# Graph network, pass 0: the last dense run's seven groups are summed from stored blocks instead of gathered rows

## The reference

```python
agg = segment_sum(x[src], dst)                    # pass 0
h1  = (agg + x) @ W1 + b1                         # 256 -> 1024
h1  = relu(batchnorm(h1) * gamma + beta)
x   = layernorm(x + relu(h1 @ W2 + b2))
deg = segment_sum(ones, dst) + 1                  # with self loops
for W, b in three layers:                         # passes 1 to 3
    h = relu(segment_sum((h @ W.T)[src] * norm, dst) + b)
out = layernorm(x + h)
```

## Time and profile before

| | |
|---|---|
| median of three runs | 2947.22 us |
| the profiled execution | 2956.98 us (its span 2955.2 us) |
| pass 0, up to the last chunk's copies | about 1106 us |
| network stage and three passes | the rest, about 1850 us |
| GpSimd in pass 0 | 832 gathers, eight per group |
| TensorE's granted clock over the span | 0.907 of full |

### The profile page before, as it was taken

The page is one execution under the profiler, slowest core; times in us unless marked ns, Lnnn a source line. Parts: engine busy times, 40 slices in busy tenths (PEclk is TensorE's granted clock), DMA queues, the critical chain, the costliest instruction groups (busy, mean ns, idle before and its releaser), DMA issues.

```text
span 2955.2 us, 44275 instructions
## 1 busy us (share of the span) xinstructions
PE 2422.4 (82%) x15812; PEld 1796.7 (61%) x15812; DVE 1422.1 (48%) x3544; ACT 956.6 (32%) x1512; POOL 2029.4 (69%) x2155
## 2 busy tenths in 40 slices
PE   3677766766676779989999987999999889999986
PEld 2444444444444457767777765777776667777764
DVE  7777787768687756751323133122222322324234
ACT  0111111111111115545444443444444344443430
POOL 6777777777777750027777776777777757777773
PEclk9987888878777879999999999999999999999997
DMA  4444554454455448987988898789898978888893
GB/s 135 137 160 143 162 159 143 160 159 159 143 162 160 142 136 272 345 282 258 321 284 290 275 335 279 243 263 306 275 309 303 316 238 263 271 272 272 259 331 105
DMA packets 361526, 681.74 MB, mean 231 GB/s; under 512 B 44243, under 2 KB 190633, under 8 KB 355403
## 3 DMA queue, kind: packets, MB, share of 16 engines
q0 software_dynamic: 103152, 296.88, 32.6%
q10 hardware_dynamic: 154688, 222.02, 22.8%
q1 hardware_dynamic: 103451, 159.81, 15.3%
HBM read 560.99 MB, written 117.51 MB: 230 GB/s over the span
## 4 chain that ended last, share of the span: by engine, by line
PE 62%; DVE 16%; DMA 9%; issue 8%; DVEq 2%; ACT 2%; SPq 0%; POOL 0%; ACTq 0%
PE ps L1058 30%; PE ps L922 9%; PE ps L904 7%; PE ps L960 6%; DVE vreg L1246 5%; DMA hbuf<-parts_d 4%; PE ps L970 4%; PE ps L1042 2%; PE ps L934 2%; DMA xs<-in_x_dram 2%; DMA xs<-x_d 2%; DVEq L1203 2%; DVE vreg L1233 1%; PE ps L947 1%; DVE vreg L1227 1%
## 5 line engine op out<-in xcount | busy, mean ns | idle before, releaser
L619 POOL DMA_INDIRECT ring<-table_d,idx x1248 | 1194.3, 957 | 443.8 <-issue 377.8
L1058 PE MATMUL ps<-wide,hbuf 128*128 128x512 f32 x4116 | 1044.1, 406 | 35.5 <-DMA hbuf<-parts_d 30.6
L619 POOL DMA_INDIRECT ring<-in_x_dram,idx x832 | 819.5, 985 | 265.9 <-issue 251.6
L1058 PEld LDWEIGHTS ps<-wide,hbuf 128*128 128x128 f32 x4116 | 763.4, 192 | 260.5 <-issue 57.0
L779 ACT CAST wide<-abuf 128x1024 fp32r<-128x1024 uint8 (+1 forms) x588 | 552.5, 940 | 636.5 <-PE ps L1058 636.5
L1199 DVE TENSOR_TENSOR acc<-acc,ps 128x256 f32 x260 | 107.6, 414 | 680.1 <-PE ps L922 678.3
L904 PE MATMUL ps<-ring,hot 128*32 128x256 f32 x4160 | 322.2, 432 | 103.0 <-issue 75.1
L922 PE MATMUL ps<-place,strips 128*128 128x128 f32 x2080 | 328.1, 308 | 66.5 <-ACT strips L666 36.2
L934 PE MATMUL ps<-vreg 128*128 128x300 bf16 x832 | 196.6, 348 | 223.0 <-DVE vreg L1246 204.0
L922 PEld LDWEIGHTS ps<-place,strips 128*128 128x128 f32 x2080 | 306.0, 219 | 107.5 <-ACT strips L666 55.9
L1246 DVE TENSOR_TENSOR vreg<-vreg,ps 128x600 f32 x416 | 326.2, 784 | 59.2 <-DVE vreg L1246 23.2
(11 more groups left out here) (131 smaller groups left out, 1541.2 us busy)
## 6 DMA issues: line engine op xcount, KB each, us to landing
hbuf<-parts_d ACTq DMA_DIRECT2D x84, 1024.0 KB
hbuf<-parts_d ACTq DMA_DIRECT2D x84, 768.0 KB
abuf<-ad_d ACTq DMA_DIRECT2D x63, 896.0 KB, 7.5
parts_d<-vreg SPq DMA_DIRECT2D x72, 512.0 KB, 5.4
h_d<-ureg SPq DMA_DIRECT2D x23, 1024.0 KB, 7.6
ureg<-h_d POOLq DMA_DIRECT2D x23, 1024.0 KB, 8.2
ad_d<-vreg SPq DMA_DIRECT2D x28, 784.0 KB, 4.2
ring<-table_d,idx POOLq DMA_INDIRECT x1248, 5.0
```

What stands on the lines that cost most here:

```text
L619: pool.indirect_dma_start(out=ring[:, i % SLOTS, j, :], out_offset=None, in_=table[0:N, :], in_offset=at).then_inc(g["rows"][i % SLOTS], 16)
L1058: ins = pe.matmul(ps[:, 2 + 4 * q + h, 0:(n1 - 4 * q) * P].rearrange("p (s n) -> p s n", n=P), hbuf[:, bl, e * D + h * P:e * D + (h + 1) * P],
```

## The change

Pass 0 no longer gathers the seven groups 84 to 90, the last dense run. Their sums come from the same four byte blocks that passes 1 to 3 use.

- The four blocks of that run are built first (`BORD`), so that they are stored early. The other 24 follow.
- `x` is split into upper and lower halves in pass 0: 49 pieces of 128 rows, two for each of the gathered groups 3 to 26 and one for group 27. SyncE loads a piece into `us`, VectorE masks and subtracts it (`split_x`, L1385 and L1388), and SyncE stores it to `xparts`.
- TensorE gets 196 steps (`quick_step`, L1083), four blocks by 49 pieces, one 128x512 matmul each into bank 5. They start at group 14, three in a turn (four in a block's first turn). The first is put ahead of the group's sums, the others behind the late tiles. ScalarE issues their loads (L835, L841) and widens the bytes (L848).
- The seven groups keep their place as turns in which only edges are counted. These are turns 23, 31, 42, 50, 61, 69 and 87 (`ORD`). In four of them (`QSUMS`) bank 5 is also copied and added to `acc` through matmuls with the identity. The 97 gathered groups stand at the turns `UNIT`.
- The 416 tile builds are spread over the 97 gathered groups. They keep their banks 2, 3, 6 and 7.
- Bank 5 is now the steps' in pass 0. So a group's strips and its sums share bank 4, and the edge counts go to bank 0, where every other pair of the hidden layer goes as well. The strips of a group must therefore wait until the group before has been added, which before only the counts behind the strips did.
- The degree row is kept in 16-bit integers. At the end of pass 0 it is loaded to `deg16`, and VectorE adds it into `deg` before TensorE transposes it.

```diff
+    QD = ND - 1
+    QGROUPS = list(range(*DENSE[QD]))
+    GATH0 = [k for k in range(NG) if k not in QGROUPS]
+    QSTART, QLEN = 14, 16
...
+    XSPLIT_AT = {UNIT[3 + b // 2]: list(range(b, min(b + 2, NB))) for b in range(0, NB, 2)}
...
+        SUMBANK, QBANK, COUNTBANK = (4, 5, 5, 5), 5, 0
...
+            for k in range(NG):
+                for b in XSPLIT_AT.get(k, ()):
+                    wait(sp, s_xst[b % 2], b // 2 * 16)
+                    sp.dma_start(xsplit(b)[0:xrows(b), D:HALVED * D], x[b * P:b * P + xrows(b), :]).then_inc(s_xq[b % 2], 16)
                 for t in BUILD_AT[k]:
                     if t in LAST:
                         store_block(LAST.index(t))
+                for b in XSPLIT_AT.get(k, ()):
+                    sp.wait_ge(s_xd, 2 * b + 2)
+                    sp.dma_start(xparts[b * P:b * P + xrows(b), :], xsplit(b)[0:xrows(b), :]).then_inc(s_xst[b % 2], 16)
...
             pool.wait_ge(s_idx, 2)
-            gather(0, x, EVERY)
+            gather(0, x, GATH0)
...
+            def quick_rows(q):
+                b = q % NB
+                wait(act, s_qstep, q - 2)
+                act.wait_ge(s_xst[b % 2], (b // 2 + 1) * 16)
+                act.dma_start(hq[:, q % 3, :].bitcast(F32), xparts[b * P:(b + 1) * P, :]).then_inc(s_qr[q % 3], 16)
+            def quick_widen(q):
...
+                wait(act, s_qstep, q - 1)
+                act.copy(wideq[:, q % 2, :], abq[:, n % 2, bl * P:(bl + 1) * P]).then_inc(s_qw, 1)
...
             def group_strips(a, i):
                 g = aggs[a]
                 pe.wait_ge(g["hot"], i + 1)
                 wait(pe, g["kept"], i)
                 if a == 0:
                     wait(pe, g["acc"], i)
+                if a > 0 or i in UNIT:
...
+                    wait(pe, fast[0]["hs"], sum(len(cs) for cs in AT0[:i]) * HP - 1)
...
+            def quick_step(q):
+                r, b = q // NB, q % NB
+                pe.wait_ge(s_qr[q % 3], (q // 3 + 1) * 16)
+                pe.wait_ge(s_qw, q + 1)
+                if b == 0 and r > 0:
+                    pe.wait_ge(aggs[0]["kept"], QSUMS[r - 1] + 1)
+                pe.matmul(ps[:, QBANK, :], wideq[:, q % 2, :], hq[:, q % 3, :],
+                          start=(b == 0), stop=(b == NB - 1)).then_inc(s_qstep, 1)
...
+            def split_x(b):
+                dve.wait_ge(s_xq[b % 2], (b // 2 + 1) * 16)
+                t = xsplit(b)[0:xrows(b), :]
+                dve.tensor_scalar(t[:, 0:D].bitcast(I32), t[:, D:HALVED * D].bitcast(I32), UPPER, None,
+                                  ALU.bitwise_and).then_inc(s_xd, 1)
+                dve.wait_ge(s_xd, 2 * b + 1)
+                dve.tensor_tensor(t[:, D:HALVED * D], t[:, D:HALVED * D], t[:, 0:D], ALU.subtract).then_inc(s_xd, 1)
...
+            dve.wait_ge(s_degl, 32)
+            dve.tensor_tensor(deg[:, :], deg[:, :], deg16[:, :], ALU.add).then_inc(s_dega, 1)
```

More of the change, by code:

```diff
@@ L12 @@
 U8 = mybir.dt.uint8
+U16 = mybir.dt.uint16
 U32 = mybir.dt.uint32
@@ L38 @@
 FRONT = 4
+PARTS = 2
+FAR = 1000
 def gnn_kernel(nc, x, src, dst, w1, b1, gamma, beta, w2, b2, wl, bl, out):
@@ L75, in gnn_kernel @@
     DLOADS = NB // BLOCKS
+    QD = ND - 1
+    QN = NSG[QD]
+    QGROUPS = list(range(*DENSE[QD]))
+    GATH0 = [k for k in range(NG) if k not in QGROUPS]
+    QSTART, QLEN = 14, 16
+    QFIRST = [QSTART + r * (QLEN + 1) for r in range(QN)]
+    counted = [q0 + QLEN // 2 for q0 in QFIRST][:len(QGROUPS) - QN]
+    ORD, UNIT, QSUMS = [], [], []
+    for n, k in enumerate(GATH0):
+        UNIT.append(len(ORD))
+        ORD.append(k)
+        if n - QLEN + 1 in QFIRST:
+            QSUMS.append(len(ORD))
+        if n - QLEN + 1 in QFIRST or n in counted:
+            ORD.append(QGROUPS[len(ORD) - len(UNIT)])
+    assert sorted(ORD) == list(range(NG)) and len(QSUMS) == QN
+    QSTEPS_AT = [[] for _ in range(NG)]
+    for q in range(QN * NB):
+        QSTEPS_AT[UNIT[QFIRST[q // NB] + q % NB * QLEN // NB]].append(q)
+    XSPLIT_AT = {UNIT[3 + b // 2]: list(range(b, min(b + 2, NB))) for b in range(0, NB, 2)}
     ENDS = [9, 23, 37, NSP - 8]
@@ L123, in bounds @@
         return least, most
-    added0 = EVERY
+    added0 = [ORD.index(k if k not in QGROUPS else QGROUPS[0] - 1) for k in range(NG)]
+    assert QSUMS[-1] <= added0[QGROUPS[0]]
     added1 = [SPARSE.index(k) if k in SPARSE else 1 + ENDS[[g0 <= k < g1 for g0, g1 in DENSE].index(True)]
@@ L334, in gnn_kernel @@
         s_bst = sem("s_bst")
+        s_xq = [sem(f"s_xq{i}") for i in range(2)]
+        s_xd = sem("s_xd")
+        s_xst = [sem(f"s_xst{i}") for i in range(2)]
+        s_ql = [sem(f"s_ql{i}") for i in range(2)]
+        s_qr = [sem(f"s_qr{i}") for i in range(3)]
+        s_qw = sem("s_qw")
+        s_qstep = sem("s_qstep")
+        s_dega = sem("s_dega")
+        s_degx = sem("s_degx")
         s_ld = [sem(f"s_ld{i}") for i in range(2)]
@@ L737, in _, with quick_sources @@
             act.wait_ge(s_srcst, 16)
-            for k in EVERY:
+            def quick_sources(n):
+                r, c = n // DLOADS, n % DLOADS * BLOCKS * P
+                wait(act, s_qw, (n - 1) * BLOCKS)
+                act.wait_ge(s_bst, 16 * (r + 1))
+                act.dma_start(abq[:, n % 2, :], ad_d[QD, :, r, c:c + BLOCKS * P]).then_inc(s_ql[n % 2], 16)
+            def quick_rows(q):
[4 more added lines that the diff above has]
+            def quick_widen(q):
+                n, bl = q // BLOCKS, q % BLOCKS
+                if bl == 0:
+                    act.wait_ge(s_ql[n % 2], (n // 2 + 1) * 16)
+                wait(act, s_qstep, q - 1)
+                act.copy(wideq[:, q % 2, :], abq[:, n % 2, bl * P:(bl + 1) * P]).then_inc(s_qw, 1)
+                if bl == BLOCKS - 1 and n + 2 < QN * DLOADS:
+                    quick_sources(n + 2)
+            for k in range(NG):
                 keep_strips(0, k)
@@ L742, in _ @@
                     act.wait_ge(s_kt, 2)
+                if k == UNIT[QSTART - 1]:
+                    for n in range(2):
+                        quick_sources(n)
+                        quick_rows(n)
+                        quick_widen(n)
+                    quick_rows(2)
+                for q in QSTEPS_AT[k]:
+                    if q + 2 < QN * NB:
+                        quick_widen(q + 2)
+                    if q + 3 < QN * NB:
+                        quick_rows(q + 3)
                 if k == 2:
@@ L1017, in _ @@
                     build(t)
+                for q in QSTEPS_AT[k][:1]:
+                    quick_step(q)
                 for c in AT0[k]:
@@ L1026, in _ @@
                     build(t)
+                for q in QSTEPS_AT[k][1:]:
+                    quick_step(q)
                 for c in AT0[k]:
@@ L1384, in _ @@
             dve.wait_ge(s_idx, 8)
-            make_hot(0, 0, 0)
+            make_hot(0, 0, ORD[0])
             dve.memset(acc[:, 0, :], 0.0)
@@ L1392, in _ @@
             dve.drain()
-            for k in EVERY:
+            for k in range(NG):
                 if k + 1 < NG:
-                    make_hot(0, k + 1, k + 1)
+                    make_hot(0, k + 1, ORD[k + 1])
                 for t in EARLY_AT[k]:
                     add_tile(t)
-                add_group(0, k, k)
+                add_group(0, k, ORD[k])
                 if k == 0:
@@ L1424, in _ @@
                     tile_hot(t)
+                for b in XSPLIT_AT.get(k, ()):
+                    split_x(b)
                 if k == 2:
```

170 lines of the change are left out of this document (111 added, 59 removed).

## The result

The changed kernel took **3021.26 us** (median of 4 runs, 3000.58 to 3025.99), the kernel before 2950.54 us (4 runs beside them, 2942.24 to 2954.80). The ratio is 1.0218, with a 95% interval of 1.0190 to 1.0245: slower, by about 71 us. The profiled execution took 3025.13 us.

The account below looks back on a forecast made before the run. The prediction took the TensorE and VectorE loop, VectorE tighter, as pass 0's limit once gathers drop. -44 + 28 + 12 + (35 - 5) + (21 - 5) - 5, with the end, gave +38 us: 2985 us, range 2915 to 3032.

Parts of the forecast that it names:

- The prediction's first step: Pass 0: with seven groups fewer to gather, the TensorE and VectorE loop limits, so at most 44 us are released.
- GpSimd stays the bound: Rival, pass 0 gathers: if the loop left alone beats 9.67 us, the gain is up to 72.5 us, or 2875; 5%.
- the loop's own pace of 9.67 us: TensorE and VectorE loop in pass 0: 9.67 us per group when not held by gathers, 0.68 us under GpSimd's pace.
- Splitting, +28: VectorE, turns 3 to 28: 49 pieces at 0.9 us make 44 us, 16 absorbed by waits for sums, rest +28.
- Transfers, +12: Piece loads and stores in pass 0: delays behind chunk transfers, 3 x 4 = +12 us.
- The slower rival: Piece transfers set the pace: load and store at 6.7 us each cost 134 in place of 40, or 3079; 9%.
- The steps, +35 less 5: TensorE's 196 matmuls at 0.3 us, partly hidden under waits for adds: +35 us, about 5 of it under the splitting.
- The bound of 70: Upper bound in us on the steps' cost on TensorE; above 59 only if each step costs more than 0.3.
- The shared bank, +21 less 5: Strips wait for the group before to be added: 26 turns x 0.81 = +21 us, some 5 under the splitting.
- Count turns, -5: Seven turns lose eight strips and four sums each but keep the engines' round: -5 us, bounds -14 and +7.
- What would show it: Profile signs: GpSimd's ring waits, last strips near 1132 us, VectorE's sum waits vanishing in turns 3 to 28, growing behind.
- the clock rises: Rival: steps keep TensorE at 2.4 GHz, speeding hidden layers (33 us) and strips (34 us): 2918; 8%.

Follow-up runs that it names:

- e1: Kernel before with the gathers of seven groups left out, all other work kept: 2890.68 us against 2953.84, ratio 0.9807.
- e12: Kernel before with four instead of eight gathers per group from the fifth on in pass 0: 2876.64 us against 2947.32, ratio 0.9764.
- e2: Changed kernel without VectorE's splitting instructions, all transfers kept: 2978.65 us against 2953.84 for the kernel before, ratio 1.0094.
- e11: Changed kernel without splitting, pieces and steps, sums and counts back in bank 5: 2898.01 us against 2952.09 for the kernel before, ratio 0.9823.
- e4: Changed kernel without the steps, their loads and widening, and with sums and counts back in bank 5: 2948.26 us, ratio 0.9988 to the kernel before.
- e3: Changed kernel without the 196 steps, their loads and widening; splitting and shared bank stay: 2976.43 us, ratio 1.0092 to the kernel before.
- e9: Changed kernel without splitting, float32 steps on rows of x placed between builds, sums and counts in bank 0: 2915.16 us against 2952.09 for the kernel before.
- e10: As e9, but one-pass 128x256 steps on rounded rows from a copy of x: 2931.34 us, ratio 0.9914 to the kernel before.
- e5: The kernel of e12, run where the kernel before itself took 3646.09 us: 3308.51 us, ratio 0.9080.

## Why the prediction was right, and where its steps were off

The direction held, the time lay in the range, and the four added parts cost time as forecast: a release of some tens of us was more than eaten up by splitting, transfers, steps and bank. The prediction had +38 us, and the medians say +71. Behind that stand two errors of opposite signs, so that the time came within 11 us of the range's upper end and not beyond it is partly luck.

**What bounds the kernel, and the release.** The prediction's first step was that the gathers are not the bound once the loop is let go, so that seven gathers fewer release 44 us. This step failed in its size: e1 released 63 us, with GpSimd waiting for hardly anything. The rival "GpSimd stays the bound" is what happened to the gathers alone (63 of its 72.5). The number at fault is the loop's own pace of 9.67 us, read from the 34 groups of the earlier trace rows. A loop that waits for no rows was taken to be at its best. e12 shows 9.35 for the same groups and 9.39 behind them.

**Splitting, +28.** e2 gives 29.6 us in the turns where it stands. That this meets the forecast is luck, for both of its parts were off. The mask and the subtraction took 286 and 426 ns, as in the earlier trace rows, but the subtraction followed with no wait between them, and the next mask began 0.66 us after the first (93.81 and 94.47). So a piece took 0.66 us and not 0.9, and 49 took 32 and not 44. Of these hardly anything was absorbed, and not 16: VectorE's waits for sums in turns 3 to 28 were 12.8 us in e11 and 13.1 in e4. By the medians, and with what comes behind turn 28, the splitting cost 43.

**Transfers, +12.** Splitting and transfers together cost 42.1 us in turns 3 to 28 (e11 to e4). Less e2's 29.6 this leaves 12.5, a difference of two differences and so a rough one; by the medians it is 50 less 43. VectorE waited 11.3 us in 6 times for a piece. The slower rival (134 us) didn't come about: the piece loads, of 128 KB, landed after a median of 3.8 us, not the 6.7 of the chunk loads of twice that size in the earlier trace rows:

```profile
DMA to landing us min/median/max: 2.3/3.8/7.5
```

**The steps, +35 less 5.** Measured: 43 us at the last add, 45 by the medians. 9 of them lie in turns 3 to 28, where 43 of the 196 steps stand, and 33 behind with the other 153: 0.21 us per step in both. The price of 0.3 us for a step that shows was too low. A step took 0.50 us in the median, at a clock of 0.76 to 0.82, and TensorE waited 21.6 us in 12 times ahead of steps for their rows. I had cost the rows at nothing, because ScalarE's queue had time. By their size these waits could be half of the 43 us, but no run takes them away. The bound of 70 held.

**The shared bank, +21 less 5.** Measured: 26 us at the last add, 28 by the medians. The mechanism is the predicted one. The strips waited for the add 31 times in e3, 29.2 us in all or 0.94 each, where the forecast had 26 times 0.81. In the changed kernel the wait shows only as 4.1 and 7.7 us, since steps cover part of it.

**Count turns, -5.** Measured together with the new distribution of tiles: +9 us at the last add (e1 to e11) and +7 by the medians, at the bound of +7 and not clear of the noise. The prediction had not costed the distribution at all.

**The sum.** Release 19 us larger than forecast; splitting and transfers 47 for 40, steps 43 for 30, bank 26 for 16, order 9 for -5, together 44 us more. The net is 24 us above the forecast at the last add. The rest of the difference to the medians is what follows pass 0 and the scatter of a few us there.

**What would show it.** The ring waits and the counts of the new instructions came as said, and the last strips came late, at 1156.6 us rather than 1132. Wrong was that VectorE's waits for sums would vanish in turns 3 to 28: they are 25.0 us in 94:402, or 0.96 per turn, more than the 0.65 of the earlier trace rows. Behind these turns they hardly grew. Over pass 0 they are 99.3 us in 94:1140, against 87.7 in 94:1080 of the kernel before:

```profile
DVE ureg L1352 <- PE ps L1063: 99.3, 74, 5.7
```

```profile
DVE ureg L1197 <- PE ps L926: 87.7, 68, 8.9
```

The near equality hides a change of cause. In the kernel before, part of these waits came from missing rows; with enough rows they are 56.5 us (e11), and bank and steps bring them back up.

**The clock.** The rival "the clock rises" didn't come about in the changed kernel. The clock fell, to 0.76 in 94:423 from 0.83. Behind turn 28 it did rise, to 0.82 from 0.79 or 0.80, far from full speed. The windows of e11, e4 and e3 for the same stretch show with which part it fell:

```profile
94.00:423.00 329.00, 227.36 (x1978) 149.12 (x1982) 260.22 (x650) 51.66 (x134) 249.17 (x251) 0.85 0.48 154
```

```profile
94.00:423.00 329.00, 213.23 (x1736) 140.58 (x1740) 258.11 (x664) 46.35 (x118) 224.90 (x227) 0.77 0.61 196
```

```profile
94.00:423.00 329.00, 219.06 (x1722) 143.63 (x1722) 251.84 (x650) 46.36 (x118) 221.57 (x223) 0.73 0.61 193
```

It is 0.85 without the added work, 0.77 with splitting and pieces, 0.73 with the shared bank too, and the steps raise it a little, to 0.76. Without the splitting, but with pieces, bank and steps (e2), it was 0.80. In e9, without splitting and with longer steps in the gaps, it was 0.89. So steps can raise the clock, as the rival had it, and in 94:423 the splitting and the bank outweighed that. The section "HAM oscillation — how this bites in real kernels" of the Trainium skill ("TensorE: Matmul & The Clock Gate"), which the prediction named, says that gaps bring the clock down and continuous work keeps it up; e11 against e4 and e9 against e10 agree with it: of the 329 us TensorE was busy 227 at 0.85 against 213 at 0.77, and 244 at 0.89 against 230 at 0.84. The kernel before does not fit in that row, with 233 us at 0.83, so busy time alone doesn't tell the clock.

## What to carry to other kernels

A pace that a loop shows while it catches up is one that it can reach, and not the best that it can do: the same 34 groups took 9.67 us each in one kernel and 9.35 in another, without waits for rows in either. Before a release is priced by it, run the kernel with the other engine's work halved, as in e12. When two engines' limits lie within a few us of one another, work moved from one to the other isn't free even where the profile shows the receiver idle: of a gain of 63 us here, 125 us of side work left a loss. Work that starts a turn should not share a bank with what the turn before ends on (28 us here). Side work is best tried in the gaps in which the engine waits anyhow, as in e9, though e9 changed the rows and the bank as well and doesn't show what the places alone are worth.

## What the runs showed of the hardware

- **More matmuls, less time.** With steps twice as long in TensorE's gaps the granted clock was 0.90 instead of 0.84, and the kernel was 16 us faster by the medians (e9 against e10; the cause is argued, not shown). Without any added work, too, the clock in 423:1023 rose from 0.80 to 0.86 once TensorE no longer waited for rows (e1).
- **The same kernel 24% slower.** 3646 us against 2950, under one and the same chip number. Halving the gathers was worth 9.2% there instead of 2.4% (e5, e12), and pass 0 with all gathers lost 309 us where that with half of them lost 40. What the difference is stays open.
- **Two dependent VectorE instructions without a gap.** The subtraction of 128x256 needs the mask's result, and started 0.31 us after the mask, which takes 0.28 (93.81 and 94.12). The add of 128x600 from PSUM waited 0.19 us for its own engine's result.
- **Loads of 256 KB land fast in a busy pass, but not evenly.** The steps' 196 loads (51 MB) landed after 3.8 us in the median at a DMA share of 0.61 to 0.71 (shortest, median and longest below, line L841). The three slots ahead did not cover the longest, and TensorE waited for rows all the same, 21.6 us in 12 times:

```profile
DMA to landing us min/median/max: 2.6/3.8/10.0
```
